# The same steps in another order: two layers of attention and feed-forward on one core, the start's transfers planned anew

## The chip, the core and the metric

One core of a Trainium2 chip. The core's engines are TensorE (PE, with its weight loads shown as PEld), VectorE (DVE), ScalarE (ACT), GpSimd (POOL) and SyncE (SP); each runs its own list of instructions, and they meet at semaphores. The metric is the device time of one execution in microseconds; of the kernel before three runs are shown, 415.20, 415.71 and 416.52, median 415.71.

## What is computed

Four sequences (batches) of 256 rows with 256 features, in float32, go through four stages. LN is a layer norm without parameters, and every stage adds its result to `x`.

```
x += softmax(LN(x) ctx^T / 16, masked) ctx                     ctx: 1601 rows per batch
x += top-2 of 8 experts, weighted: (silu(h Wg) * (h Wu)) Wd    h = LN(x), chosen by softmax(h Wr)
x += softmax(the 54 largest of coef (LN(x) Wq^T) ctx^T) ctx Wo^T
x += bitlinear(gelu(bitlinear(LN(x), w1)), w2)                 8-bit activations, ternary weights
```

## The kernel before, in words

The 1,024 rows are eight tiles `t` of 128 rows (two to a batch). `ctx` is cut in four column chunks `c` for scores and in four units `u` (three of 512 rows, one of 65) for the product with the values. `x` is loaded and normalised in pairs of tiles, the rows `u` of `ldx`, `stats`, `norm` and `xT`.

The whole program is one list, `ORDER`, of steps such as `s1.0.2`. Each engine's block walks this list and emits the steps that are its own; a step of another engine is passed over. So the list fixes the order of each engine's instructions, and nothing else does: the semaphore waits are worked out from it (`n(op, *key)` is the number of steps of that name up to this one). The rings of buffers follow the list too: two score banks (`s1`, `s3`, `up`), two transpose banks, one bank `O` for all small products, one accumulator `A`.

The steps that matter here, with their lines:

- On SP, all in list order through one queue: `ldx.u` (L468, 256 KB of x), `ldk.l.b.c` (L484, 400 KB of transposed ctx: layer l, batch b, chunk c; for b above 0 it waits until both tiles of the batch before have used that chunk), `ldv.l.a.u` (L502, 512 KB of ctx rows, 65 KB for the last unit), `fixed` (L470 to L473: two weight matrices and four scalars), `zero` (L476, fills the 1,920 KB DRAM array `xs` with zeros), `wg`, `wd` (L527, L534, expert weights), `xgl` (L510, loads a tile of gathered rows), `yst` (L515, stores an expert's output).
- On ACT, which also issues some loads: the first mask (L627) and the router weights (L628) ahead of the list, `mask.b` (L637, turns the byte mask into an additive one; then it issues the next batch's mask load, L641), `wload` (L706, L709), `wqa` (L720, mean magnitude of a weight matrix), `xTe`, `pTe` (L655, L670, copies out of a transpose bank), `exp1`, `exp3` (L661, L751), `egap` (L696), `qTe` (L729), `silu`, `ye`, `xgTe`, `gelu`, `gmul`, `aTe`, `cent`, `h4e`. Exponential, silu and gelu need different tables, and a change of table is an ACT_TABLE_LOAD.
- On TensorE: `xT`, `pT`, `xgT`, `q4`, `h4T` (transposes), `s1.t.c` and `s3.t.c` (scores, L905; the bank must be free, that is the `s1e` two chunks earlier must be done), `pvm.l.t.u` (values, L932 for layer 1, L936 for layer 3), `router`, `rank`, `GU`, `down` (experts), `wqs` (L999), `qT`, `wo`, `up`, `dn`.
- On VectorE: `stats`, `aggr`, `var`, `norm`, `s1e` (L1106, adds the mask and keeps the maximum), `max1`, `x1` (L1126), `rt1`, `rt2`, `pos` (routing), `mul` (L1197), `upd` (L1218), `wqb` (L1235 to L1243, the weight quantisation), and for layer 3 the search for the 54-th largest score: `pairH`, `pairL` fold a row of 1601 in two halves, `maxH`, `repH`, `maxL`, `repL` (L1260 to L1277) take eight values at a time out of each half, `merge`, `thr` find the threshold, `cut` (L1296) applies it; `x3` (L1312), `xabs` (L1318), `gabs`, `fin` (L1365).
- On POOL: the constants, `rstd` (L576), `scat` (L586, scatters the rows to `xs` by expert, only when `zero` has landed), `gat` (L597, gathers the experts' outputs, only when all `yst` have landed).

The rows of a batch of layer 1 wait for its mask: the first `s1e` of tile 0 needs `mask.0`. In `wqa` and `wqb` the array `w_raw` is rows 2 and 3 of `row3`.

Of the kernel before, what the change touches and what calls it, by code (L numbers as in the profile page):

```python
# [18 lines left out]
P = 128  # L19
# [54 lines left out]
fixed exp1.1 pvm.1.0.1 pT.1.0.2 ldv.1.0.3 pTe.1.0.2 s1.2.2 pT.1.1.0 ldk.3.0.0 pT.1.0.3 pvm.1.0.2 pTe.1.1.0 s1e.2.2  # L74
s1e.2.0 pT.1.1.1 s1.2.1 pTe.1.1.1 pTe.1.0.3 coef_e rstd.1.3 ldk.3.0.3 s1e.2.1 s1.3.1 pvm.1.0.3 r1.0 pT.1.1.2 pT.1.1.3
s1.2.3 x1.0 s1e.2.3 s1e.3.1 pvm.1.1.0 max1.2 s1.3.2 ldk.1.2.2 pvm.1.1.1 s1e.3.2 pTe.1.1.2 pTe.1.1.3 pvm.1.1.2
ldv.1.1.0 s1.3.0 pvm.1.1.3 x1.1 ldk.1.2.1 ldv.1.1.3 ldv.1.1.1 stats.2.0 exp1.2 aggr.2.0 pT.1.2.0 s1.3.3 var.2.0
pTe.1.2.0 s1e.3.0 s1e.3.3 xT.1.2 pT.1.2.1 max1.3 pvm.1.2.0 pTe.1.2.1 ldv.1.1.2 ldv.3.0.3 ldk.1.2.0 xTe.1.2 mask.2
rstd.2.0 s1.4.1 pT.1.2.2 exp1.3 ldk.1.2.3 pTe.1.2.2 pvm.1.2.1 norm.2.0 s1.4.2 pT.1.2.3 s1e.4.2 pTe.1.2.3 s1e.4.1
pvm.1.2.2 pT.1.3.0 pT.1.3.1 r1.1 pvm.1.2.3 norm.1.3 pTe.1.3.0 pTe.1.3.1 s1.4.3 pT.1.3.2 x1.2 wload.2 pTe.1.3.2 s1e.4.3  # L80
pvm.1.3.0 pT.1.3.3 s1.4.0 pvm.1.3.1 s1e.4.0 max1.4 xT.2.0 pvm.1.3.2 ldv.1.2.2 pTe.1.3.3 ldv.1.2.1 exp1.4 pvm.1.3.3
wqa.2 s1.5.3 x1.3 ldk.1.3.3 stats.2.1 aggr.2.1 xTe.2.0 ldv.1.2.0 var.2.1 s1e.5.3 router.0 pT.1.4.0 s1.5.1 rstd.2.1
norm.2.1 s1.5.0 ldk.1.3.0 rt1.0 s1e.5.1 xT.2.1 pTe.1.4.0 ldk.1.3.1 s1e.5.0 s1.5.2 s1e.5.2 ldk.1.3.2 xTe.2.1 pT.1.4.1
ldv.1.2.3 router.1 rt1.1 xT.1.3 max1.5 pvm.1.4.0 rank.0 mask.3 pTe.1.4.1 pos.0 xTe.1.3 pT.1.4.2 pT.1.4.3 pTe.1.4.3
pvm.1.4.1 s1.6.2 exp1.5 scat.0.0 scat.1.1 wg.0.0 pTe.1.4.2 s1e.6.2 pT.1.5.0 pT.1.5.1 wd.0.0 egap.0 pvm.1.4.2 scat.3.0
rt2.0 wqs.2 r1.2 pTe.1.5.0 pT.1.5.2 pvm.1.4.3 s1.6.0 ldk.3.0.2 wg.0.1 x1.4 scat.0.1 scat.2.1 scat.1.0 pTe.1.5.1
scat.3.1 wd.0.1 pT.1.5.3 s1e.6.0 pTe.1.5.2 wg.0.2 pvm.1.5.0 s1.6.1 s1.7.1 pvm.1.5.1 s1e.6.1 scat.2.0 xgl.0.0 pvm.1.5.2
s1.6.3 xgT.0.0 s1e.7.1 xgl.0.1 ldv.1.3.0 xgl.0.2 pTe.1.5.3 pvm.1.5.3 wqb.2 xgT.0.1 xgTe.0.0 GU.0.0 xgTe.0.1 x1.5
xgT.0.2 stats.2.2 xgl.0.3 wd.0.2 aggr.2.2 var.2.2 xgl.0.5 rstd.2.2 silu.0.0 ldv.1.3.2 mul.0.0 GU.0.1 norm.2.2 s1e.6.3
s1.7.3 xgl.0.4 silu.0.1 s1e.7.3 ldv.1.3.1 mul.0.1 max1.6 xgTe.0.2 xgT.0.3 down.0.0 xgTe.0.3 GU.0.2 wg.0.3 xgl.0.6  # L90
xgT.0.5 ye.0.0 down.0.1 wd.0.3 silu.0.2 wg.0.4 xgT.0.4 xgTe.0.4 xgl.0.8 mul.0.2 ye.0.1 wd.0.4 GU.0.3 silu.0.3 down.0.2
yst.0.0 xgTe.0.5 wg.0.5 ye.0.2 mul.0.3 s1.7.2 GU.0.4 wd.0.5 exp1.6 yst.0.1 xgl.0.7 wg.0.6 down.0.3 yst.0.2 wd.0.6
xgT.0.6 xgl.0.9 silu.0.4 xgTe.0.6 ye.0.3 GU.0.5 silu.0.5 wg.0.7 mul.0.4 down.0.4 xgT.0.7 wd.0.7 pT.1.6.0 ye.0.4
mul.0.5 GU.0.6 xgTe.0.7 down.0.5 pTe.1.6.0 wg.0.8 xgT.0.8 xgTe.0.8 silu.0.6 yst.0.3 yst.0.4 ye.0.5 mul.0.6 GU.0.7
wd.0.8 xgl.0.11 xgl.0.10 xgT.0.9 xgTe.0.9 wg.0.9 yst.0.5 silu.0.7 down.0.6 wd.0.9 xgl.0.13 GU.0.8 mul.0.7 ye.0.6
s1e.7.2 s1.7.0 xgT.0.11 wg.0.10 down.0.7 xgl.0.12 silu.0.8 s1e.7.0 wd.0.10 GU.0.9 max1.7 wg.0.11 xgTe.0.11 mul.0.8
xgT.0.10 ye.0.7 silu.0.9 xgTe.0.10 pT.1.6.1 down.0.8 yst.0.6 egap.1 GU.0.10 yst.0.7 wd.0.11 mul.0.9 ye.0.8 down.0.9
exp1.7 wg.0.12 wd.0.12 GU.0.11 silu.0.10 pTe.1.6.1 mul.0.10 pT.1.6.2 wg.0.13 ye.0.9 xgT.0.12 down.0.10 xgl.0.14
silu.0.11 yst.0.8 xgTe.0.12 ye.0.10 mul.0.11 GU.0.12 wd.0.13 pTe.1.6.2 silu.0.12 wg.0.14 yst.0.9 xgT.0.13 xgTe.0.13
mul.0.12 down.0.11 GU.0.13 wd.0.14 xgT.0.14 ye.0.11 ldk.3.0.1 silu.0.13 down.0.12 xgTe.0.14 yst.0.10 ldv.1.3.3 rt2.1  # L100
yst.0.11 GU.0.14 mul.0.13 ye.0.12 down.0.13 silu.0.14 yst.0.12 pT.1.7.0 mul.0.14 ye.0.13 coef pT.1.6.3 down.0.14 r1.3
yst.0.13 ye.0.14 yst.0.14 pvm.1.6.0 pTe.1.7.0 pvm.1.6.1 xT.2.2 xTe.2.2 pvm.1.6.2 gat.0.0 pTe.1.6.3 ldv.3.0.0 gat.1.0
pvm.1.6.3 router.2 x1.6 gat.0.1 pT.1.7.1 upd.0.0 rt1.2 pT.1.7.2 gat.1.1 pvm.1.7.0 upd.1.0 upd.0.1 pTe.1.7.1 gat.2.0
pT.1.7.3 upd.1.1 pTe.1.7.3 pTe.1.7.2 pvm.1.7.1 gat.3.0 egap.2 stats.3.0 pvm.1.7.2 aggr.3.0 var.3.0 rstd.3.0 upd.2.0
norm.3.0 gat.3.1 pvm.1.7.3 upd.3.0 gat.2.1 x1.7 xT.3.0 xTe.3.0 stats.2.3 qT.0 aggr.2.3 var.2.3 rstd.2.3 upd.3.1 qTe.0
norm.2.3 upd.2.1 xT.2.3 s3.0.2 xTe.2.3 stats.3.1 aggr.3.1 var.3.1 router.3 rt2.2 s3e.0.2 s3.0.1 rt1.3 rank.1 rstd.3.1
s3e.0.1 norm.3.1 s3.0.0 s3.0.3 pos.1 xT.3.1 egap.3 scat.4.0 s3e.0.0 wg.1.0 rt2.3 scat.7.1 s3.1.2 ldk.3.1.2 s3e.0.3
pairH.0 s3e.1.2 s3.1.3 s3.1.0 scat.4.1 scat.7.0 pairL.0 maxH.0.0 xTe.3.1 s3e.1.3 maxL.0.0 ldk.3.1.0 repH.0.0 s3.1.1
repL.0.0 ldk.3.1.1 ldk.3.1.3 maxH.0.1 scat.5.0 scat.5.1 qT.1 s3e.1.1 s3e.1.0 scat.6.1 wd.1.0 qTe.1 maxL.0.1 s3.2.0
wg.1.1 s3.2.1 s3e.2.0 s3.2.3 pairH.1 s3e.2.1 s3.2.2 scat.6.0 repL.0.1 s3e.2.3 repH.0.1 wd.1.1 maxH.1.0 nmax.1 maxH.0.2  # L110
xgl.1.0 pairL.1 repH.1.0 repH.0.2 s3e.2.2 xgl.1.1 s3.3.0 xgl.1.2 maxL.1.0 maxH.0.3 xgT.1.0 xgl.1.3 maxH.1.1 xgT.1.1
xgTe.1.0 wg.1.2 xgl.1.4 xgTe.1.1 GU.1.0 xgT.1.2 GU.1.1 wd.1.2 repH.0.3 wg.1.3 ldk.3.2.0 repH.1.1 silu.1.0 xgT.1.3
mul.1.0 xgTe.1.2 s3.3.3 repL.1.0 xgl.1.5 xgTe.1.3 down.1.0 silu.1.1 maxH.0.4 ye.1.0 maxL.1.1 xgT.1.4 mul.1.1 xgl.1.6
wd.1.3 GU.1.2 repH.0.4 down.1.1 silu.1.2 maxH.1.2 mul.1.2 xgTe.1.4 nmax.0 GU.1.3 ye.1.1 xgT.1.5 wg.1.4 wd.1.4 down.1.2
# [1279 lines left out]
```

## Time and profile before

| | |
|---|---|
| runs, median (lowest to highest) | 415.71 us (415.20 to 416.52) |
| the profiled execution | 416.91 us |
| its span, first to last instruction | 415.2 us |
| mean granted TensorE clock | 0.971 |
| DMA over the span | 76.39 MB, mean 184 GB/s |
| instructions | 6,609 |

A row of a timeline has the start in us from the span's start, the duration in us, the engine, the line, the operation, what it writes and reads, the shapes, and how many instructions were merged in it; in brackets stands how long the engine was idle before it and what ended that. An engine with a q behind its name is its queue, issuing. Matmul ends are modelled. A row of groups has the busy time in us, the mean duration in ns of one, and the idle time before them.

### The profile page before, as it was taken

To read this page: it belongs to the slowest core of one execution; us is meant where nothing else is said; L and a number is where in the kernel's file an instruction comes from. 1 tells how busy PE (TensorE), PEld (TensorE's weight loads), DVE (VectorE), ACT (ScalarE), POOL (GpSimd) and SP (SyncE) were. 2 spreads that over 40 slices of the span, in tenths; PEclk is the share of its full clock that TensorE was granted. 3 is DMA by queue.
4 is the path that set the end of the run, shared out by engine and by line. 5 is a ranking of instruction groups with operands and counts; after the bars stand their busy time and mean duration, and the time that the engine had idled before them with its cause. 6 is when DMAs were issued, how large, how long until landed. Compare 5 with 4: busy or idle time off the path is not lost. (4 is left out here: it accounts for less than half of the span.)

```text
span 415.2 us, 6609 instructions
## 1 busy us (share of the span) xinstructions
PE 354.7 (85%) x2075; PEld 281.2 (68%) x2082; DVE 287.1 (69%) x701; ACT 186.9 (45%) x338; POOL 55.7 (13%) x132
## 2 busy tenths in 40 slices
PE   1899999999999999898998998879976754578884
PEld 1367778786888888564887997755953642567762
DVE  2363242745312124799798999999999998999843
ACT  1353254441373733232336373535555365543495
POOL 3100000052000005452000000451001002000110
PEclk9999999999999999998999999999999988689899
DMA  7978363857999974148797998651540230133311
GB/s 228 381 234 265 129 213 103 306 164 253 315 298 302 306 223 134 32 149 297 223 304 250 276 326 263 199 176 39 178 146 15 64 109 13 51 108 103 100 35 51
DMA packets 70810, 76.39 MB, mean 184 GB/s; under 512 B 5356, under 2 KB 69496, under 8 KB 70776
## 3 DMA queue, kind: packets, MB, share of 16 engines
q1 hardware_dynamic: 65912, 67.80, 51.9%
q0 software_dynamic: 1536, 4.20, 3.0%
q10 hardware_dynamic: 3328, 3.97, 2.8%
q8 instruction: 17, 0.28, 0.3%
q14 instruction: 17, 0.14, 0.1%
HBM read 66.91 MB, written 9.04 MB: 183 GB/s over the span
## 5 line engine op out<-in xcount | busy, mean ns | idle before, releaser
L983 PE MATMUL GU<-xgT,wg_ring 128*128 128x128 f32 x480 | 59.2, 276 | 2.8 <-ACT xgT L677 1.6
L983 PEld LDWEIGHTS GU<-xgT,wg_ring 128*128 128x128 f32 x480 | 56.8, 192 | 6.4 <-issue 3.3
L670 ACT ACTIVATE pT<-T 128x512 f32<-128x512 f32 (+1 forms) x64 | 32.1, 513 | 61.7 <-PE T L919 46.7
L936 PE MATMUL A<-pT,v_sb 128*128 128x128 f32 (+1 forms) x416 | 56.3, 293 | 3.9 <-DMA v_sb<-ctx 2.1
L936 PEld LDWEIGHTS A<-pT,v_sb 128*128 128x128 f32 (+1 forms) x416 | 53.4, 207 | 7.8 <-issue 3.9
L1260 DVE MAX8 cand_h<-fold 128x8 f32<-128x801 f32 x56 | 54.4, 983 | 0.0
L905 PE MATMUL S<-k_sb,xT 128*128 128x400 f32 (+2 forms) x128 | 50.8, 531 | 3.8 <-DMA k_sb<-ctxT 3.4
L905 PE MATMUL S<-k_sb,qT 128*128 128x400 f32 (+2 forms) x128 | 49.0, 528 | 4.0 <-DMA k_sb<-ctxT 1.9
L932 PE MATMUL A<-v_sb,pT 128*128 128x256 f32 (+1 forms) x208 | 49.0, 379 | 0.0
L1272 DVE MATCH_REPLACE8 fold<-cand_h,fold 128x801 f32<-128x801 f32 x48 | 46.9, 978 | 0.0
L1106 DVE CUSTOM_DVE_ANT_0 row<-S,mask_add 128x400 f32<-128x400 f32 (+2 forms) x32 | 18.1, 574 | 38.3 <-PE S L905 29.4
L919 PE MATMUL T<-ident,row 128*128 128x128 f32 (+1 forms) x208 | 32.7, 282 | 12.4 <-DVE row L1296 7.0
L932 PEld LDWEIGHTS A<-v_sb,pT 128*128 128x128 f32 (+1 forms) x208 | 38.2, 190 | 6.7 <-issue 0.4
L905 PEld LDWEIGHTS S<-k_sb,qT 128*128 128x128 f32 x128 | 24.5, 200 | 21.1 <-issue 6.4
L1197 DVE TENSOR_TENSOR hid<-hid,GU 128x256 f32<-128x256 f32 x30 | 12.6, 418 | 36.9 <-ACT hid L684 36.9
L919 PEld LDWEIGHTS T<-ident,row 128*128 128x128 f32 (+1 forms) x208 | 25.3, 146 | 18.9 <-issue 10.3
L905 PEld LDWEIGHTS S<-k_sb,xT 128*128 128x128 f32 x128 | 24.6, 202 | 19.2 <-DMA k_sb<-ctxT 5.0
L993 PE MATMUL O<-wd_ring,hid 128*128 128x256 f32 x120 | 31.2, 383 | 1.8 <-ACT y_sb L691 1.7
L1267 DVE MAX8 cand_l<-fold 128x8 f32<-128x801 f32 x32 | 31.4, 984 | 0.0
L597 POOL DMA_INDIRECT yg<-ys,idx_u x16 | 15.7, 981 | 88.7 <-DMA ys<-y_sb 83.2
L740 ACT ACTIVATE row<-S 128x400 f32<-128x400 f32 (+2 forms) x32 | 15.9, 503 | 24.7 <-PE S L905 24.7
L993 PEld LDWEIGHTS O<-wd_ring,hid 128*128 128x128 f32 x120 | 20.6, 190 | 4.8 <-ACT y_sb L691 2.8
(157 smaller groups left out, 460.3 us busy)
## 6 DMA issues: line engine op xcount, KB each, us to landing
v_sb<-ctx SPq DMA_DIRECT2D x36, 512.0 KB, 4.2
wg_ring<-Wg SPq DMA_DIRECT2D x30, 256.0 KB, 3.4
wg_ring<-Wu SPq DMA_DIRECT2D x30, 256.0 KB, 4.3
wd_ring<-Wd SPq DMA_DIRECT2D x30, 256.0 KB, 4.2
k_sb<-ctxT SPq DMA_DIRECT2D x16, 400.0 KB, 5.0
xg<-xs SPq DMA_DIRECT2D x30, 128.0 KB, 3.7
ys<-y_sb SPq DMA_DIRECT2D x30, 128.0 KB, 4.3
k_sb<-ctxT SPq DMA_DIRECT2D x8, 402.0 KB, 5.2
```

Of the source, the lines that this page charges most:

```text
L670: act.activation(pT[0:r, i % NPT, :, :].rearrange("p a s -> p (a s)")[:, 0:w], t_bank("pT", *key)[0:r, 0:w], ACT.Copy).then_inc(pTe_done, 1)
L740: act.activation(row3[:, t % 4, c0:c0 + w], s_bank("s3", t, c)[:, 0:w], ACT.Copy) \
L905: mm = pe.matmul(s_bank(*step)[:, 0:w], lhs[:, k, :], k_sb[:, l // 2, c, k, 0:w], start=k == 0, stop=k == KC - 1)
L919: mm = pe.transpose(t_bank(*step)[0:r, a * P:(a + 1) * P], src[:, m * P:m * P + r], ident[:, :])
L932: mm = pe.matmul(A_bank[:, 0:D], pT[0:r, j, a, :], v[0:r, a, :], start=m == 0, stop=m == NMC - 1)
L936: mm = pe.matmul(A_bank[:, o * P:(o + 1) * P], v[0:r, a, o * P:(o + 1) * P], pT[0:r, j, a, :], start=m == 0 and o == 0, stop=m == NMC - 1 ...
L983: mm = pe.matmul(gu_bank(*key)[:, a * F + f * P:a * F + (f + 1) * P], wg_ring[:, w % NWG, a, k, f * P:(f + 1) * P], cols[:, k, :], start=k ...
L993: mm = pe.matmul(O_bank[:, 0:D], hid[:, i % NHID, f, :], wd_ring[:, w % NWD, f, :], start=f == 0, stop=f == F // P - 1)
L1106: dve.tensor_tensor_reduce(out=row1[:, t % 2, c0:c0 + w], in0=s_bank("s1", t, c)[:, 0:w], in1=mask_add[:, c0:c0 + w], scale=1.0, scalar=BE ...
L1260: dve.max(cand_h[:, t % 2, 8 * r:8 * r + 8], fold[:, t % 2, 0:HALF]).then_inc(maxH_done, 1)
L1267: dve.max(cand_l[:, t % 2, 1 + 8 * r:9 + 8 * r], fold[:, t % 2, HALF:RW]).then_inc(maxL_done, 1)
L1272: dve.match_replace(part, cand_h[:, t % 2, 8 * r:8 * r + 8], part, BELOW_ALL).then_inc(repH_done, 1)
```

## The change

All steps of `ORDER` stand in another order; the set of steps is the same. One load is moved outside the list: the router weights are issued behind the conversion of the first mask instead of ahead of the list.

```diff
         def _(act):
             act.wait_ge(x_in[0], 16)
             act.dma_start(mask_u8[:, :], mask[0:1, :].partition_broadcast(P)).then_inc(mask_in, 16)
-            act.dma_start(wr_sb[:, :, :], Wr.rearrange("(k p) e -> p k e", p=P)).then_inc(wr_in, 16)
...
                     act.activation(mask_add[:, 0:M], mask_u8[:, :], ACT.Copy, scale=-NEG, bias=NEG) \
                        .then_inc(mask_done, 1)
+                    if b == 0:
+                        act.dma_start(wr_sb[:, :, :], Wr.rearrange("(k p) e -> p k e", p=P)).then_inc(wr_in, 16)
```

The list's beginning, to the first steps of batch 1, before and after:

```diff
-ldx.0 stats.1.0 ldx.2 ldk.1.0.3 ldx.3 ldk.1.0.1 ldk.1.0.0 ldk.1.0.2 ldx.1 zero wload.1 aggr.1.0 var.1.0 rstd.1.0
-norm.1.0 ldv.1.0.0 stats.1.2 aggr.1.2 xT.1.0 xTe.1.0 s1.0.1 mask.0 s1e.0.1 ldv.1.0.1 s1.0.2 stats.1.1 s1.0.0 s1e.0.2
-wqa.1 aggr.1.1 var.1.1 stats.1.3 wqs.1 rstd.1.1 var.1.2 s1e.0.0 rstd.1.2 norm.1.1 s1.0.3 s1e.0.3 s1.1.2 aggr.1.3
-max1.0 s1e.1.2 s1.1.1 s1.1.0 exp1.0 pT.1.0.0 ldk.1.1.1 s1e.1.1 ldk.1.1.0 s1e.1.0 s1.1.3 ldk.1.1.2 xT.1.1 pTe.1.0.0
-ldv.1.0.2 s1e.1.3 pT.1.0.1 norm.1.2 xTe.1.1 max1.1 ldk.1.1.3 wqb.1 ldv.3.0.1 mask.1 pvm.1.0.0 var.1.3 pTe.1.0.1 s1.2.0
-fixed exp1.1 pvm.1.0.1
+ldx.0 stats.1.0 aggr.1.0 var.1.0 rstd.1.0 norm.1.0 xT.1.0 xTe.1.0 ldx.2 ldk.1.0.3 ldk.1.0.1 s1.0.1 ldk.1.0.2 s1.0.2
+mask.0 ldx.3 ldx.1 ldk.1.0.0 ldv.1.0.0 fixed stats.1.2 stats.1.1 s1e.0.1 ldv.1.0.1 s1.0.0 s1e.0.2 s1e.0.0 s1.0.3
+aggr.1.1 var.1.1 stats.1.3 s1.1.2 s1e.0.3 rstd.1.1 aggr.1.2 max1.0 norm.1.1 ldv.1.0.3 ldv.1.0.2 s1e.1.2 s1.1.1 s1e.1.1
+exp1.0 aggr.1.3 var.1.3 s1.1.0 ldk.1.1.0 pT.1.0.0 s1e.1.0 ldk.1.1.1 s1.1.3 s1e.1.3 pTe.1.0.0 ldk.1.1.3 xT.1.1 pT.1.0.1
+ldk.1.1.2 ldk.3.0.1 xTe.1.1 max1.1 exp1.1 pvm.1.0.0 var.1.2 rstd.1.2 pTe.1.0.1 s1.2.0
```

The places of the new list that are spoken of below (with what stands between):

```
pvm.1.1.3 pTe.1.2.0 s1.3.0 x1.1 s1.3.3 s1e.3.0 ldv.1.1.1 pT.1.2.1 stats.2.0 aggr.2.0 wqs.1 s1e.3.3 ldk.1.2.3 xT.1.2
xTe.1.2 pvm.1.2.0 pTe.1.2.1 wqb.1 mask.2 ldk.1.2.0 ldv.1.1.2 pT.1.2.2 ldv.1.1.3 zero ldv.3.0.1 pT.1.2.3 s1.4.1
pTe.1.2.3 var.2.0 max1.3 rstd.2.0 s1.4.2 exp1.3 wload.2 r1.1 pTe.1.2.2 pvm.1.2.1 s1e.4.1 pvm.1.2.2
...
down.0.12 xgTe.0.14 GU.0.14 yst.0.11 ye.0.12 mul.0.13 yst.0.12 ldv.1.3.1 down.0.13 pT.1.6.3 silu.0.14 mul.0.14
ye.0.13 pT.1.7.0 down.0.14 yst.0.13 ye.0.14 yst.0.14 gat.0.0 pvm.1.6.0 ldk.3.0.0 pTe.1.6.3 ldv.3.0.3 gat.0.1 pvm.1.6.1
...
norm.3.0 xT.3.0 gat.3.1 x1.7 xTe.3.0 stats.2.3 qT.0 aggr.2.3 var.2.3 rstd.2.3 upd.3.0 egap.2 qTe.0
...
aTe.4 ldv.3.5.1 s3.7.3 s3e.7.3 repL.5.2 ginv.2 wo.4 gmul.2 maxH.5.5 xdeq.3 x3.4 h4T.2 cent.4 repH.5.5 h4e.2
```

## Rows read from the trace of the kernel before

**Rows 1.** The page's parts 1 and 2, busy time and bandwidth by slice
```profile
PE 354.7 (85%) x2075; PEld 281.2 (68%) x2082; DVE 287.1 (69%) x701; ACT 186.9 (45%) x338; POOL 55.7 (13%) x132
...
GB/s 228 381 234 265 129 213 103 306 164 253 315 298 302 306 223 134 32 149 297 223 304 250 276 326 263 199 176 39 178 146 15 64 109 13 51 108 103 100 35 51
```

**Rows 2.** Windows by stage: length; busy PE, PEld, DVE, ACT, POOL; clock; DMA share; GB/s
```profile
0.00:30.00 30.00, 19.01 (x59) 11.03 (x59) 12.50 (x49) 9.77 (x10) 5.38 (x51) 1.00 0.85 278
30.00:180.30 150.30, 146.62 (x823) 118.45 (x824) 59.63 (x237) 62.00 (x118) 21.66 (x24) 1.00 0.66 213
180.30:393.20 212.90, 174.03 (x1069) 140.51 (x1073) 206.24 (x390) 98.62 (x187) 26.89 (x50) 0.94 0.53 164
393.20:415.20 22.00, 14.99 (x128) 11.19 (x128) 8.70 (x26) 16.55 (x26) 1.78 (x8) 0.99 0.16 54
```

**Rows 3.** Timeline of all engines, 0 to 30 us
```profile
9.69 3.03 PE L905 MATMUL S<-k_sb,xT 128*128 128x400 f32 x4 [1.37 <-DMA k_sb<-ctxT]
...
11.10 1.54 ACT L637 ACTIVATE mask_add<-mask_u 128x1601 bf16<-128x1601 uint8 x1 [2.15 <-DMA mask_u<-mask]
...
14.78 4.90 PE L905 MATMUL S<-k_sb,xT 128*128 128x400 f32 x8 [2.06 <-DMA k_sb<-ctxT]
...
22.29 1.63 ACT L661 ACTIVATE row<-row,nm 128x1601 f32<-128x1601 f32 x1 [4.15 <-DVE nm L1114]
```

**Rows 4.** Timeline of TensorE, 24 to 60 us
```profile
30.00 1.59 PE L905 MATMUL S<-k_sb,xT 128*128 128x402 f32 x4 [0.33 <-issue]
...
37.65 2.85 PE L905 MATMUL S<-k_sb,xT 128*128 128x400 f32 x8
...
45.73 3.61 PE L932 MATMUL A<-v_sb,pT 128*128 128x256 f32 x16
```

**Rows 5.** DMA issues of 0 to 30 us: KB each, median us to landing
```profile
v_sb<-ctx SPq DMA_DIRECT2D x4, 512.0 KB, 8.4
xs<-zeros SPq DMA_DIRECT2D x1, 1920.0 KB, 16.5
...
row<-w1T ACTq DMA_DIRECT2D x1, 1024.0 KB, 11.5
```

**Rows 6.** The tile k_sb, 0 to 30 us: DMA to landing
```profile
DMA to landing us min/median/max: 3.2/5.9/10.9
```

**Rows 7.** Timeline of VectorE, 28 to 60 us: the quantisation's passes
```profile
28.96 1.29 DVE L1241 TENSOR_SCALAR row<-row,wscl 128x2048 f32<-128x2048 f32 x1
...
31.55 1.23 DVE L1243 TENSOR_SCALAR w1q<-row 128x2048 bf16<-128x2048 f32 x1
```

**Rows 8.** Timeline of TensorE, 80 to 110 us
```profile
102.14 0.41 PE L967 MATMUL T<-ident,xg 128*128 128x128 f32 x2 [0.67 <-DMA xg<-xs]
```

**Rows 9.** Timeline of all engines, 150 to 182 us
```profile
150.64 4.81 SPq L515 DMA_DIRECT2D ys<-y_sb  x3
...
153.56 1.13 PE L993 MATMUL O<-wd_ring,hid 128*128 128x256 f32 x4 [0.20 <-ACT y_sb L691]
...
168.32 0.63 PE L890 MATMUL T<-ident,xn 128*128 128x128 f32 x4
...
171.75 0.69 ACT L729 ACTIVATE qT<-O,scal 128x512 f32<-128x512 f32 x1 [2.16 <-PE O L1009]
```

**Rows 10.** DMA issues of the whole run: KB each, median us to landing
```profile
v_sb<-ctx SPq DMA_DIRECT2D x36, 512.0 KB, 4.2
```

**Rows 11.** Timeline of ScalarE, 216 to 224 us
```profile
220.46 1.28 ACT L751 ACT_TABLE_LOAD   x1
221.76 1.63 ACT L751 ACTIVATE fold<-row,nmax 128x1601 f32<-128x1601 f32 x1
```

**Rows 12.** Timeline of VectorE, 199 to 226 us
```profile
223.49 1.89 DVE L1296 SCALAR_TENSOR_TENSOR row<-row,thr,fold 128x1601 f32<-128x1601 f32 x1 [1.33 <-ACT fold L751]
```

**Rows 13.** Timeline of VectorE, 340 to 347 us
```profile
341.56 0.47 DVE L1312 SCALAR_TENSOR_TENSOR x_res<-O,r,x_res 128x256 f32<-128x256 f32 x1
...
345.31 0.42 DVE L1318 TENSOR_REDUCE xabs<-xn 128x1 f32<-128x256 f32 x1 [1.34 <-ACT xn L765]
```

More of the change, by code:

```diff
@@ L74 @@
[L74 to L113, printed above, removed]
@@ L129 @@
-pTe.3.1.1 repL.2.2 ldv.3.1.3 down.1.13 ldk.3.2.3 silu.1.14 yst.1.12 rc3.1 mul.1.14 repH.3.0 ye.1.13 maxL.2.3 pT.3.1.2
-yst.1.13 down.1.14 ye.1.14 pvm.3.1.0 yst.1.14 ldv.3.1.2 maxH.2.6 repL.3.0 merge.2 maxH.3.1 thr.2 gat.4.0 maxL.3.1
-repH.3.1 repL.3.1 wo.0 pTe.3.1.2 pT.3.1.3 pvm.3.1.1 pvm.3.1.2 pTe.3.1.3 gat.5.0 maxH.3.2 exp3.2 cut.2.0 gat.4.1
-upd.4.0 x3.0 ldv.3.2.0 pvm.3.1.3 pT.3.2.0 upd.4.1 upd.5.0 repH.3.2 gat.5.1 upd.5.1 maxH.3.3 pT.3.2.1 aTe.1 sq4.0 wo.1
-gat.6.0 pTe.3.2.0 pTe.3.2.1 stats.3.2 gat.7.0 gat.6.1 upd.6.0 pvm.3.2.0 aggr.3.2 ldv.3.2.3 x3.1 var.3.2 cent.0 rc3.2
@@ new lines @@
+x1.0 pTe.1.1.0 s1e.2.3 s1.2.1 pTe.1.1.1 rstd.1.3 s1e.2.1 s1.3.1 pvm.1.1.0 max1.2 exp1.2 pT.1.1.2 s1.3.2 pTe.1.1.2
+pT.1.1.3 wqa.1 ldk.1.2.2 s1e.3.1 s1e.3.2 ldk.1.2.1 pvm.1.1.1 pT.1.2.0 pvm.1.1.2 ldv.1.1.0 pTe.1.1.3 pvm.1.1.3
+pTe.1.2.0 s1.3.0 x1.1 s1.3.3 s1e.3.0 ldv.1.1.1 pT.1.2.1 stats.2.0 aggr.2.0 wqs.1 s1e.3.3 ldk.1.2.3 xT.1.2 xTe.1.2
+pvm.1.2.0 pTe.1.2.1 wqb.1 mask.2 ldk.1.2.0 ldv.1.1.2 pT.1.2.2 ldv.1.1.3 zero ldv.3.0.1 pT.1.2.3 s1.4.1 pTe.1.2.3
+var.2.0 max1.3 rstd.2.0 s1.4.2 exp1.3 wload.2 r1.1 pTe.1.2.2 pvm.1.2.1 s1e.4.1 pvm.1.2.2 s1e.4.2 norm.2.0 pT.1.3.0
@@ new lines @@
+pTe.1.3.0 pvm.1.2.3 pT.1.3.1 pTe.1.3.1 s1.4.0 pT.1.3.2 s1e.4.0 s1.4.3 x1.2 pvm.1.3.0 s1e.4.3 pTe.1.3.2 max1.4 pT.1.3.3
+pTe.1.3.3 xT.2.0 pvm.1.3.1 ldv.1.2.0 wqa.2 coef_e exp1.4 ldk.3.0.3 pvm.1.3.2 ldv.1.2.1 pvm.1.3.3 s1.5.3 x1.3 stats.2.1
+s1.5.1 ldv.1.2.3 aggr.2.1 ldk.1.3.3 s1e.5.3 xTe.2.0 norm.1.3 ldk.3.0.2 s1.5.2 var.2.1 s1e.5.1 rstd.2.1 norm.2.1
+router.0 pT.1.4.0 ldv.1.2.2 xT.2.1 rt1.0 xTe.2.1 pTe.1.4.0 s1.5.0 router.1 s1e.5.2 ldk.1.3.1 xT.1.3 pvm.1.4.0 rt1.1
+xTe.1.3 s1e.5.0 ldk.1.3.0 rank.0 pT.1.4.1 pos.0 pT.1.4.2 mask.3 ldk.1.3.2 pTe.1.4.1 s1.6.0 s1.6.2 wg.0.0 scat.0.0
@@ new lines @@
+ye.1.14 repH.3.0 yst.1.14 pT.3.1.1 merge.2 repL.3.0 pTe.3.1.1 pT.3.1.2 pT.3.1.3 maxH.3.1 pvm.3.1.1 ldv.3.1.2 gat.4.0
+thr.2 maxL.3.1 ldk.3.2.1 gat.4.1 exp3.2 pTe.3.1.3 repH.3.1 wo.0 repL.3.1 gat.5.0 upd.4.0 pTe.3.1.2 ldv.3.2.0 gat.5.1
+x3.0 sq4.0 cut.2.0 pvm.3.1.2 va4.0 gat.6.0 maxH.3.2 upd.5.0 pvm.3.1.3 rs4.0 ldv.3.2.3 pT.3.2.0 aTe.1 pT.3.2.1
+pTe.3.2.0 upd.4.1 wo.1 ldv.3.2.1 gat.7.1 cent.0 upd.5.1 pvm.3.2.0 repH.3.2 stats.3.2 maxH.3.3 aggr.3.2 x3.1 gat.7.0
+ldk.3.2.3 var.3.2 pTe.3.2.1 repH.3.3 pvm.3.2.1 sq4.1 rstd.3.2 ldv.3.2.2 norm.3.2 maxH.3.4 xT.3.2 xTe.3.2 gat.6.1
@@ new lines @@
+maxL.3.2 pT.3.2.2 qT.2 repH.3.4 qTe.2 va4.1 pTe.3.2.2 rs4.1 s3.4.0 upd.6.0 maxH.3.5 repL.3.2 cent.1 s3e.4.0 xabs.0
+ldv.3.3.0 upd.6.1 pT.3.2.3 s3.4.1 s3.4.2 repH.3.5 upd.7.0 xabs.1 maxL.3.3 s3e.4.1 upd.7.1 s3e.4.2 s3.4.3 xmx.1
+maxH.3.6 xdeq.1 xmx.0 stats.3.3 pvm.3.2.2 s3e.4.3 merge.3 pairH.4 pTe.3.2.3 aggr.3.3 xinv.1 thr.3 rc3.2 maxH.4.0
+s3.5.1 var.3.3 pairL.4 exp3.3 rstd.3.3 xdeq.0 s3.5.0 cut.3.0 nmax.4 s3e.5.1 norm.3.3 pvm.3.2.3 repH.4.0 s3.5.2
+maxL.4.0 ldv.3.3.1 xinv.0 s3e.5.0 xT.3.3 s3.5.3 pT.3.3.0 s3e.5.3 ldv.3.3.3 maxH.4.1 xTe.3.3 aTe.2 pTe.3.3.0 ldk.3.3.1
```

124 lines of the change are left out of this document (75 added, 49 removed).

## The prediction

> **What bounds the kernel now.** The page's busy times come first [rows 1]: TensorE 85%, VectorE 69%, neither enough alone. The windows by stage split the run [rows 2]. From 30 to 180.3 us TensorE is busy 146.6 of 150.3 us while VectorE has 59.6: TensorE's list is the clock. From 180.3, where the first `pairH` (the start of the 54-th-largest search) stands, to 393.2 VectorE is busy 206.2 of 212.9 us. The last 22 us are a dependent tail in which neither is full. In the first 30 us the two are busy for only 19.0 and 12.5 us. So the time is: start, TensorE's list to `pairH.0`, VectorE's list to the last `xscl`, tail. Next I read the start's timeline and the transfers issued in it, because there the new list differs most, and last the idle times named at single instructions inside the two full stretches.
>
> At the start the reader sees TensorE wait for keys, run its first score chunk at 9.69, stop, and resume at 14.78, again behind keys [rows 3]. It runs cold: four products span 3.03 us and four more take about as long, while warm ones follow each other at about 1.34 (two take 2.85 with the last one's end, [rows 4]). The transfers explain it: beside the first batch's keys a 1,024 KB weight load went over ACT's queue and took 11.5 us to land, and behind them stood a 1,920 KB fill (16.5 us) [rows 5].
>
> **The change part by part.** Which step an instruction belongs to follows from the list, because each engine runs its steps in that order; I counted the instructions out of the trace and summed their steps again in the new order.
>
> (a) The sets. TensorE does the same steps ahead of its first `s3` in both lists, VectorE the same ones ahead of `pairH.0` and ahead of `merge.7`. No instruction count changes. So only idle time can change, and I go through the places where it can.
>
> (b) The start. New: `xT.1.0 s1.0.1 s1.0.2 s1.0.0 s1.0.3`, keys 1 and 2 are the fourth and fifth loads, the weight load and the fill are gone from this stretch. Chunk 1's keys now end 1,311 KB into SP's queue instead of 1,567; 256 KB at the 381 GB/s of [rows 1] are 0.7 us, so they land at about 9.0, not 9.7. Chunk `s1.0.1` then runs cold from 9.1 to 12.0, `s1.0.2` follows without a stop and warms on the way (old TensorE was at the short step about 3.9 us after 14.78), to 13.9. The mask's conversion (11.10 plus 1.54, [rows 3]) still opens the first `s1e` at 12.8 and its transfer is not moved, so the bank for `s1.0.0` is free at 13.4; `s1.0.0` ends 15.3, `s1.0.3` 16.6, `s1.1.2` 18.0. VectorE now holds things up: `s1e.0.0` (0.6), `aggr.1.1`, `var.1.1`, `stats.1.3` (1.2 together), `s1e.0.3` end at 17.8, then `aggr`, `max1.0`, `norm.1.1` (1.4) and `s1e.1.2` end at 19.7, and `s1.1.0` waits for this bank until 19.8. `exp1.0` needs 1.8 [rows 3] after `max1.0`, so `pT.1.0.0` starts at 21.1, and with one chunk, two transposes of 0.45 and so on `pvm.1.0.0` starts near 24.2 and ends at 25.9. `s1.2.0` needs batch 1's keys, sent when `s1.1.0` is done at 21.1; the quickest key transfer of the stretch took 3.2 us, the median 5.9 [rows 6]. The queue is empty by then, I take 3.2 to 4.5: `s1.2.0` starts at 25.9 instead of 30.00 [rows 4]. The old list had also run `wqs.1` (0.5) by then, so the head start is 4.1 - 0.5 = **3.6 us**. Bounds: 5.0 if VectorE's pieces overlap better, 1.3 if TensorE stays cold for one chunk more (1.3) and the keys take 5.9 (about 1 more).
>
> (c) The weight quantisation `wqb.1` moves from 28.5 us, where VectorE was idle afterwards, to between `s1e.3.3` and `max1.3`. Its three passes take 1.29, 1.23 and 1.23 [rows 7], about 4.3 with the small ones. TensorE has from the end of `s1.3.3` to `pvm.1.2.2`: two full groups of transposes, one of a single tile and an `xT` (1.4), two value units of 1.72 (two take 3.61 in [rows 4]), two chunks of 1.34, `wqs` 0.15, together 7.7. The chain: a 0.3 us late `s1e.3.3` (0.6), `wqb.1` 4.3, `var` and `max1.3` 0.5, `exp1.3` 1.8, `pTe` 0.6, four hand-overs 0.5: 8.7. **Cost 1.0 us**; bounds 0 and the whole 4.3.
>
> (d) Smaller waits of the same kind in the new list ahead of `rank.0`: `s1.3.1` behind `x1.0` and `s1e.2.3` (0.3), `s1.5.2` behind `x1.3`, `stats`, `aggr`, `s1e.5.3` (0.2 over before): **0.5**. New waits of 0.4 to 0.5 between `rank.0` and `xgT.0.0` cost nothing: there eight scatters end at a landing for which TensorE waited before too [rows 8], and TensorE's work between is 17.4 instead of 17.1 us. In the feed-forward stretch `egap.0` and `egap.1` and one exp stand together ahead of `silu.0.10`: **0.4**. Bounds for (d) together: 0 and 2.
>
> (e) The fill, now sent near 50 us, stands behind all keys and values of its neighbourhood, and its first user, the scatters, come 30 us later; the transfers were at two thirds of their time there [rows 2]. Its cover is that distance; 16.5 us would still fit. `wload.1` has no user before `wqa.1`. Cost 0. Router weights: one 8 KB load goes behind the mask's conversion; it has 50 us until `router.0`, and the second mask's load behind it has over 10. Cost 0. SP now issues `fixed` (six loads) ahead of values 1, 3 and 2; SP has nothing due until 21 us.
>
> (f) Behind `down.0.14` (153.56 plus 1.1) the path runs over the store, the gathers, `upd`, `norm.3.0` to `xT.3.0` at 168.32 [rows 9]; TensorE's own work between is as long, 13.5 us, in both lists. New is that `ldv.1.3.1` (512 KB) is sent behind `yst.0.12`, at old times 151.1, with the stores of [rows 9]. With the 4.2 us that value loads usually take [rows 10] it lands at 155.3, before `pvm.1.6.1` at 156.0. Cost 0; upper bound below. Also new: `egap.2` with its table load stands between `xTe.3.0` and `qTe.0`. A load of 1.28 [rows 11] and 0.2 for `egap` fit into the 2.16 us for which ACT waited ahead of `qTe.0` [rows 9]. The Trainium skill says otherwise: "ScalarE: Activation LUTs", What ACT_TABLE_LOAD costs, gives every switch a drain of about 1.38 us beside the load's 1.28. By that `qTe.0` would come 0.7 us later and the sum would be 2.0 faster instead of 2.7; here the exponential begins right at the load's end (220.46 + 1.28, 221.76), so the trace does not agree. The new list has 20 such loads instead of 18; ACT is busy 98.6 of 212.9 us [rows 2] and the two lie off VectorE's path.
>
> (g) VectorE's full stretch. The distance of every `mul`, `cut`, `gabs` and `xabs` from what it waits for is within 0.5 us of before up to `cut.0.0`, whose wait of 1.33 stays [rows 12]. The wait of 1.34 at 345 [rows 13] and one of 0.37 behind it came from `x3.4` (341.56) standing just 2.7 us of VectorE work ahead of `xabs.4`; now 8.5 stand between. In return `aTe.4` comes behind two exponentials, and `x3.4` is wanted 5.6 us sooner. I take **1.0 gained** of the 1.7; bounds 1.7 and a loss of 1. The tail has the same chain, `wo.7 cent.7 h4e.4` to `dn.7`: 0, with 0.7 either way.
>
> Sum: -3.6 + 1.0 + 0.5 + 0.4 - 1.0 = -2.7 us. The profiled execution took 416.91 (span 415.2), 1.2 above the median of 415.71; the sum is a difference, so profiled 414.2 and median **413.0**.
>
> **The rivals.** *1, all of it arrives.* TensorE reaches `wqb.1` with its waits taken up by others, and both waits at 345 go: -3.6 - 1.7 = -5.3, 410.4. For: small waits seldom add. Against: VectorE has no slack around `wqb.1`. 15%. *2, the start gives little.* Keys or cold TensorE as in the bound of (b): -1.3 + 1.9 - 1.0 = -0.4, 415.3. For: every load there takes longer than later, 8.4 against 4.2 us for values [rows 5, 10]. 20%. *3, slower: the late value load.* If `ldv.1.3.1` takes the 8.4 us of [rows 5] it lands 3.5 us after `pvm.1.6.1` is due, and as TensorE's work there is as long as the path, all 3.5 count: -2.7 + 3.5 = +0.8, and with 0.5 for the last store and gathers queued behind it +1.3, 417.0. It decides above 4.9 us from issue; the gain is gone at 7.6. The transfers are near full in the stretch before. 13%. *4, the switch.* If a table load keeps ACT twice as long as its row (2.56), `qTe.0` is 0.6 late: 413.6. 5%. "ScalarE: Activation LUTs" of the Trainium skill is the page that would have it so. The forecast itself has 47%, with 410.9 to 415.0 as its own range.
>
> **How the numbers follow.** Faster by over 0.3% (1.25 us, about what a measurement of this kernel can tell from no change): 0.42 of the forecast, rivals 1 and 4, 0.02 of rival 2: 0.64. Within: 0.04 + 0.16 = 0.20. Slower: 0.01 + 0.02 + 0.13 = 0.16. Range 410.5 to 416.6: it holds the forecast, rivals 2 and 4 and the near half of 1.
>
> **What the new profile would show.** (b) right: TensorE's second chunk without a stop at 12, `s1.2.0` near 26. (c) right: a wait of about 1 us of the transposes' copy for `exp1.3` near 55. `pairH.0` near 178.6 instead of 180.3, the end of VectorE's stretch near 390.5. Wrong if TensorE still stops for keys after its first chunk, if `pvm.1.6.1` waits for v_sb, or if `xabs.4` still waits.

## The result, and the profile after

| | before | after |
|---|---|---|
| runs of this comparison, median (lowest to highest, 20 each) | 417.3 us (415.18 to 421.72) | 412.98 us (409.18 to 419.04) |
| ratio after to before, 95% interval | | 0.9881 (0.9857 to 0.9905) |
| the profiled execution, its span | 416.91 us, 415.2 us | 413.82 us, 412.1 us |
| mean granted TensorE clock | 0.971 | 0.959 |
| ACT busy, table loads | 186.9 us, 18 | 190.4 us, 20 |

The changed kernel is 1.2% faster: 0.0119 of 417.3 is 5.0 us. The ratio leaves disturbed runs out, so it is not quite the quotient of the two medians, 0.9896. The two profiled executions differ by 3.1 us only. The one of before took 0.4 less than its median, the one of after 0.8 more, so the traces show the direction of each part better than its size.

A second profiled execution of the changed kernel (called the second trace below; it is the run new_again) had a span of 410.3. Windows of the first one, cut where the same steps stand as in [rows 2] (columns as there):

```profile
0.00:30.00 30.00, 22.00 (x78) 14.11 (x79) 10.41 (x44) 10.54 (x12) 6.03 (x52) 1.00 0.79 250
30.00:175.80 145.80, 141.35 (x803) 115.02 (x802) 60.90 (x241) 60.68 (x116) 21.39 (x23) 1.00 0.70 225
175.80:389.80 214.00, 175.33 (x1079) 141.70 (x1084) 206.25 (x391) 103.33 (x187) 30.43 (x51) 0.93 0.51 164
389.80:412.10 22.30, 15.34 (x119) 10.84 (x119) 8.63 (x26) 15.87 (x25) 1.55 (x7) 0.92 0.13 44
```

The first `pairH` stands at 175.8 instead of 180.3. TensorE's idle time from 30 us to it is 4.45 us (145.80 less 141.35), before it was 3.68 [rows 2]. So the stretch that TensorE's list sets is not shorter, it only begins earlier, and the gain was made in the first 25 us. From `pairH` to the start of the last-but-one `xscl` it is 214.0 us where before it was 212.7 (that `xscl` starts at 393.0; the window of [rows 2] is cut 0.2 behind it). The tail, 22.3 from there, was 22.2, but its clock is 0.92 where it was 0.99.

TensorE's start (timeline of the changed kernel; the answer to [rows 3] and the second row of [rows 4]):

```profile
9.09 11.62 PE L906 MATMUL S<-k_sb,xT 128*128 128x400 f32 x28 [0.78 <-ACT xT L656]
...
24.92 1.51 PE L906 MATMUL S<-k_sb,xT 128*128 128x402 f32 x4
```

Seven chunks run as one row from 9.09, where before TensorE stopped for keys at 12.7 and began again at 14.78. The second chunk's first weight load is at 11.2 and `s1.2.0`, the second row, at 24.9 (its weight load at 24.7), against 30.00. The end of the list has a new wait on VectorE, for `x3.6`:

```profile
384.18 0.48 DVE L1313 SCALAR_TENSOR_TENSOR x_res<-O,r,x_res 128x256 f32<-128x256 f32 x1 [1.76 <-PE O L1018]
```

The wait at `xabs.4` [rows 13] is gone: in the timeline of the changed kernel it follows at once on what stands ahead of it.

```profile
340.61 0.17 DVE L1286 TENSOR_TENSOR split_min<-cand_h,cand_l 128x28 f32<-128x28 f32 x1
340.70 0.41 DVE L1319 TENSOR_REDUCE xabs<-xn 128x1 f32<-128x256 f32 x1
```

### The profile page after: what moved, and what is told of

Same layout as the page of the kernel before. It is cut to its first block, busy times and chain, and to the rows that moved or that the text cites. A ratio compares the mean times of both kernels' runs of the same rounds, so it can differ in the third digit from the quotient of the medians.

```text
span 412.1 us, 6611 instructions
## 1 busy us (share of the span) xinstructions
PE 354.0 (86%) x2075; PEld 281.7 (68%) x2082; DVE 286.2 (69%) x701; ACT 190.4 (46%) x340; POOL 59.4 (14%) x132
## 4 chain that ended last, share of the span: by engine, by line
PE 43%; DVE 23%; issue 12%; DMA 11%; SPq 4%; POOL 3%; ACT 3%; POOLq 0%; ACTq 0%; DVEq 0%
PE S L906 11%; PE GU L984 8%; PE A L933 8%; DVE fold L1273 5%; DVE cand_h L1261 5%; PE O L994 4%; DMA ys<-y_sb 4%; PE T L920 3%; DMA xs<-xn,idx_u 3%; PE A L937 2%; POOL xs L586 2%; DVE cand_l L1268 2%; DMA xg<-xs 2%; DVE fold L1278 2%; SPq L527 2%
## 5 line engine op out<-in xcount | busy, mean ns | idle before, releaser
L906 PE MATMUL S<-k_sb,xT 128*128 128x400 f32 (+2 forms) x128 | 48.3, 518 | 0.8 <-ACT xT L656 0.8
L920 PE MATMUL T<-ident,row 128*128 128x128 f32 (+1 forms) x208 | 33.7, 286 | 10.1 <-DVE row L1297 9.8
L906 PEld LDWEIGHTS S<-k_sb,qT 128*128 128x128 f32 x128 | 23.4, 196 | 21.9 <-ACT row L741 5.9
L920 PEld LDWEIGHTS T<-ident,row 128*128 128x128 f32 (+1 forms) x208 | 26.1, 148 | 16.9 <-issue 12.7
L906 PEld LDWEIGHTS S<-k_sb,xT 128*128 128x128 f32 x128 | 24.2, 198 | 15.9 <-issue 3.2
L741 ACT ACTIVATE row<-S 128x400 f32<-128x400 f32 (+2 forms) x32 | 15.9, 502 | 25.2 <-PE S L906 25.2
```

The source lines that it names most:

```text
L906: mm = pe.matmul(s_bank(*step)[:, 0:w], lhs[:, k, :], k_sb[:, l // 2, c, k, 0:w], start=k == 0, stop=k == KC - 1)
L920: mm = pe.transpose(t_bank(*step)[0:r, a * P:(a + 1) * P], src[:, m * P:m * P + r], ident[:, :])
```

## The experiments

All twelve were timed in five rounds against the kernel before, in three groups, each on one chip. The order is that of the questions. Where a kernel is said to differ in "places", these are places in the one list of steps; no step is added or left out anywhere.

**Where was it made?** First the changed kernel once more.

> The changed kernel itself, timed beside the splices on one chip. If the ratio of its first measurement holds, 0.988; if the gap between its two profiled executions (3.1 us) is the truth, 0.9925. In either case its first pairH stands near 175.8 us; what a second trace can tell is whether TensorE's clock drops again in the last 10 us.

Measured: 412.11 us, ratio 0.9874 (0.9816 to 0.9931), where the kernel before has a median of 418.39. `pairH.0` at 175.4, and the clock fell again at the end. The result holds.

Then the two lists were spliced. The first half of the first pair:

```diff
-(old list)
+(new list up to s1.2.0) (the rest of the old list in its own order)
```

> New list up to s1.2.0, then the old list's remaining steps in the old order; router weights as in the new kernel. Theory A (all of the gain is made in the first 25 us and carried through TensorE's full stretch): s1.2.0 near 24.7, the first pairH near 175.5 to 176, and a time 4 to 5 us below the kernel before. Rival B (the gain comes from the rest of the list, and a head start is given back at the next wait): pairH near 179 to 180, 0 to 1.5 us below.

Measured: 424.37 us, ratio 1.0133 (1.0085 to 1.0180), slower than both. `s1.2.0` was at 24.8, so the start was won. Then TensorE stood still (its timeline, the only row with a wait from 24 to 62 us):

```profile
34.22 0.59 PE L1000 MATMUL O<-wabs,ones 128*128 128x2 f32 x2 [7.73 <-ACT gel L721]
```

The steps that the new start puts off, the weight load, its mean and its sum `wqs.1`, came first in the rest, so TensorE waited 7.73 us for a matrix that had only just been asked for. The splice was made badly for my question; what it does show is that a head start lasts to the first step whose input was put off further than the step itself.

The other half:

```diff
-(new list)
+(old list up to s1.2.0) (the rest of the new list in its own order)
```

> Old list up to s1.2.0, then the new list's remaining steps in the new order. Theory A: s1.2.0 stays at 30.0, the first pairH comes at 180 to 181, and the time is within 1 us of the kernel before, or up to 1.5 us slower because the new order behind pairH has about 1.3 us more waits. Rival B: 2 to 4 us faster.

Measured: 417.15 us, ratio 0.9977 (0.9936 to 1.0017): no change that can be told from none. `s1.2.0` was at 28.0 in this trace and `pairH.0` at 178.2, 150.2 us behind it, where the kernel before has 150.3. By itself the new order behind the start gives at most 2.7 us, by the interval's lower end, and in the trace nothing ahead of `pairH.0`.

That `s1.2.0` stands at 28.0 here and not at 30.0, with the same list up to it, matters for what the start is worth. The stop for keys is there too, but the two chunks behind it took 2.96 us, where they took 4.90 before [rows 3] (TensorE's timeline):

```profile
14.09 2.96 PE L905 MATMUL S<-k_sb,xT 128*128 128x400 f32 x8 [1.78 <-DMA k_sb<-ctxT]
```

So 1.9 of the 5.3 us between 30.0 and 24.7 are TensorE's slow pace behind the stop in that one trace of the kernel before, and not the stop.

A splice at a place where both lists have done nearly the same steps:

```diff
-(old list)
+(new list up to s1.4.2) (the rest of the old list in its own order)
```

> The splice made again where the two lists agree better: new list up to s1.4.2 (with the weight load, its mean and its quantisation at the new places, 6 us of TensorE's work after s1.3.3), the old order behind it. Theory A (the gain is the start): s1.2.0 near 25, first pairH near 176 to 177, pairH to last-but-one xscl 212 to 213, time 4 to 5 us below the kernel before, within 1 us of the changed kernel. Rival B (the gain needs the new order of the feed-forward stretch): pairH at 178 or later and at most 2 us below the kernel before.

Measured: 418.14 us, ratio 1.0017 (0.9976 to 1.0057). By its numbers this is rival B, by the place of the loss it is not. `s1.2.0` at 25.2 and `s1.4.1` at 51.3 are those of the changed kernel, and `pairH.0` is at 179.8; but already `router.1`, ahead of the feed-forward stretch, stands at 78.8 where the kernel before has 80.1, so that of the 4.8 us won 1.3 are left. TensorE's timeline, the window over it (columns of [rows 2]) and ScalarE's timeline show the larger part of the loss:

```profile
70.91 1.03 PE L947 MATMUL O<-wr_sb,xT 128*128 128x8 f32 x8 [1.14 <-issue]
...
72.53 4.28 PE L906 MATMUL S<-k_sb,xT 128*128 128x400 f32 x8
```

```profile
66.00:82.00 16.00, 14.86 (x74) 10.82 (x73) 7.61 (x40) 7.05 (x10) 0.69 (x1) 0.89 0.66 223
```

```profile
68.33 1.91 ACT L721 ACTIVATE gel<-row 128x2048 f32<-128x2048 f32 x1 [1.46 <-DMA row<-w2T]
70.14 0.19 ACT L721 ACTIVATION_READ_ACCUMULATOR gel<-row 128x1 f32 x1
70.24 0.58 ACT L656 ACTIVATE xT<-T 128x512 f32<-128x512 f32 x1
```

The first router product waited 1.14 us (1.8 counted from the last weight load) for ScalarE's copy of `xT`, which stands behind the mean of the second weight matrix, and that one waited 1.46 us for its load. The splice sends this load at 59.3, when the moved fill (50.3 to 61.3) was still under way, and it landed at 68.3, 9 us later; the kernel before sends it at 63.1 and has it at 68.4, the new list sends it at 53.1. And behind that stop the granted clock of the stretch is 0.89 and the eight products of a chunk pair take 4.28 us, where eight take 2.85 in [rows 4]: 1.4 us more. Together that is 3.2 us of the 4.3 by which the way from `s1.2.0` to `pairH.0` is longer than before (154.6 against 150.3).

Last of this group, only the second half of the run in the old order:

```diff
-(new list)
+(new list up to s3.0.2) (the rest of the old list in its own order)
```

> New list up to s3.0.2, the old order behind it. Theory A (the new order of VectorE's stretch and of the tail is worth nothing or costs about 1.3 us): first pairH near 175.8, then old behaviour, 393.0 - 180.3 = 212.7 us from pairH to the last-but-one xscl as before, so 0 to 1.5 us below the new kernel in the traces, 411 to 412 us. Rival C (the new order behind pairH has gained, as the prediction's step (g) said by 1.0): 1 us above the new kernel.

Measured: 413.21 us, ratio 0.9871 (0.9812 to 0.9929), where the changed kernel beside it has 412.11 and 0.9874. The two can't be told apart, but each interval reaches 2.4 us either way, so the runs rule out neither the 1 us of gain of rival C nor as much of loss. What they do show is that the gain over the kernel before does not need the new order of VectorE's stretch and of the tail.

**What made the start short?** The first try put both bulk transfers back:

```diff
-ldx.3 ldx.1 ldk.1.0.0 ldv.1.0.0
+ldx.3 ldx.1 zero wload.1 ldk.1.0.0 ldv.1.0.0
```

> The new list with the 1,920 KB fill and the 1,024 KB weight load put back behind the start's loads of x, all else new. Theory S (the bulk transfers share the wires with the keys and hold SP's queue, and that is what made the old start long): the mask, keys 0 and the first values land 2 to 4 us later than in the new kernel, s1.0.0 or pvm.1.0.0 waits, s1.2.0 comes at 27 to 29 instead of 24.7 to 25.5, time 2 to 4 us above the new kernel. Rival K (the order of the keys alone made the gain, since TensorE needs keys 3 and 1 first): s1.2.0 stays within 1 us of 25, time within 1 us of the new kernel.

Measured: 423.58 us, ratio 1.0154 (1.0101 to 1.0208), `s1.0.0` at 22.3 and `s1.2.0` at 34.8. It overshoots, because the fill now stood ahead of keys 0 in SP's queue, which it did not in the old list. So again, with the fill behind the keys and the weight load at the head of ACT's list:

```diff
-ldx.0 stats.1.0
+ldx.0 wload.1 stats.1.0
...
-ldk.1.0.0 ldv.1.0.0
+ldk.1.0.0 zero ldv.1.0.0
```

> The new list with the weight load at its very start on ACT's queue, as before, and the fill behind the last of the first batch's keys (ahead of values 0). The first try had put the fill ahead of keys 0, which the old list did not. Theory S (bulk beside the keys makes the start long): keys 1 and 2 land 1 to 4 us later, TensorE stops for them as in the old kernel, values 0 land 4 us or more late, s1.2.0 at 27 to 30 and the time 2 to 4 us above the new kernel. Rival K (the order of the keys made the gain): s1.2.0 within 1 us of 25.2.

Measured: 416.64 us, ratio 1.0005 (0.9964 to 1.0046). With the order of the new list and the bulk where it was, no gain is left that the ratio can show. (By the medians of all runs, 416.64 against 418.39 of the kernel before, 1.7 us of it may be.) Within this group it is 3.3 us slower than `tail_mended`, 413.33, which is the changed kernel but for six steps near the end. TensorE's timeline:

```profile
9.11 5.35 PE L906 MATMUL S<-k_sb,xT 128*128 128x400 f32 x8 [0.78 <-ACT xT L656]
16.27 7.00 PE L906 MATMUL S<-k_sb,xT 128*128 128x402 f32 x20 [1.82 <-DVE mx1c L1107]
...
28.87 1.59 PE L906 MATMUL S<-k_sb,xT 128*128 128x402 f32 x4 [1.22 <-issue]
```

Keys 1 and 2 were in time, so the old stop behind the first chunk does not come back: that half of theory S failed, the new order of the loads alone is enough against it. But TensorE started its third chunk 2.7 us late (16.3 against 13.6 in the run below), and `s1.2.0` came at 28.8. The row says that the third chunk waited for VectorE's release of its bank. VectorE's timeline tells why:

```profile
14.98 0.75 DVE L1071 BATCH_NORM_STATS2 bn<-x_res 128x6 f32<-128x256 f32 x2 [7.22 <-DMA x_res<-x]
15.65 0.56 DVE L1107 CUSTOM_DVE_ANT_0 row<-S,mask_add 128x400 f32<-128x400 f32 x1
```

`stats.1.1`, which stands ahead of `s1e.0.1`, waited for rows 1 of `x`, landed at 14.96 beside the weight load (12.30 without it, in the run below), and the bank's reader could only follow. Keys 0 landed at 16.05 instead of 13.39, so they would have held the chunk as long. SP's own timeline shows the second half of it:

```profile
5.48 0.57 SPq L476 DMA_DIRECT2D xs<-zeros  x1
6.10 9.75 SPq L502 DMA_DIRECT2D v_sb<-ctx  x1
15.89 1.81 SPq L470 DMA_DIRECT2D wq_sb<-WqT  x1
...
23.30 2.67 SPq L484 DMA_DIRECT2D k_sb<-ctxT  x4
```

The issue of values 0 behind the fill took 9.75 us, and all that SP had to send stood behind it. In the changed kernel the same issue takes 0.48:

```profile
5.27 0.48 SPq L502 DMA_DIRECT2D v_sb<-ctx  x1
...
20.73 3.17 SPq L484 DMA_DIRECT2D k_sb<-ctxT  x5
```

The fill alone:

```diff
-ldk.1.0.0 ldv.1.0.0
+ldk.1.0.0 zero ldv.1.0.0
```

> The new list with the fill alone put back, behind keys 0 and ahead of values 0; the weight load stays late. If the weight load beside the keys is what stops TensorE's second chunk, this run starts as the new kernel does (s1.0.2 at 11.2), and only values 0 and what SP sends behind them are late: pvm.1.0.0 waits for v_sb. If the values land by 24 all the same, s1.2.0 stays within 1 us of 25.2 and the time within 1 us of the new kernel.

Measured: 414.33 us, ratio 0.9944 (0.9910 to 0.9978): 2.3 us faster than with both put back, 1.0 slower than `tail_mended` in the same group.

```profile
9.11 11.51 PE L906 MATMUL S<-k_sb,xT 128*128 128x400 f32 x28 [0.78 <-ACT xT L656]
...
26.82 1.59 PE L906 MATMUL S<-k_sb,xT 128*128 128x402 f32 x4 [1.83 <-issue]
```

```profile
6.70 6.53 SPq L502 DMA_DIRECT2D v_sb<-ctx  x1
...
20.65 3.50 SPq L484 DMA_DIRECT2D k_sb<-ctxT  x5
```

The first seven chunks are those of the changed kernel (values 0, landed at 21.0, were in time). What is late are the keys of batch 1: sent at the same time, 20.65, they landed 6.1 us later (26.73) instead of 3.3, because the 1.1 MB of values sent from 17.8 on, and not from 11.3, stood ahead of them. `s1.2.0` is at 26.8 after a wait of 1.83 us. So of the 3.6 us by which `s1.2.0` fell behind with both put back, the fill makes some 1.6 and the weight load beside the keys the other 2.

The converse, the bulk alone taken out of the old start:

```diff
-ldx.1 zero wload.1 aggr.1.0
+ldx.1 aggr.1.0
...
+mask.1 wload.1
...
-ldv.1.1.3 ldv.1.1.1
+ldv.1.1.3 zero ldv.1.1.1
```

(and `wqa.1`, `wqs.1`, `wqb.1` between the steps that they stand between in the new list)

> The old list with the weight load behind mask.1, the fill behind ldv.1.1.3, and the mean, the sum and the quantisation of that weight behind it as in the new list; keys, loads of x and all else as in the old one. Theory S: the start loses its stop for keys, s1.2.0 at 25 to 27 instead of 28 to 30, and the time is 2 to 4 us below the kernel before. Rival K: s1.0.2 still waits (x 2 and 3 and the keys' order are as before), s1.2.0 at 28 or later.

Measured: 423.28 us, ratio 1.0172 (1.0111 to 1.0234). The start does what theory S says: `s1.0.2` at 12.6 instead of 14.8, `s1.2.0` at 26.2. The time does not follow, for two waits of TensorE for values:

```profile
39.55 0.70 PE L932 MATMUL A<-v_sb,pT 65*128 65x256 f32 x2 [2.52 <-DMA v_sb<-ctx]
...
60.45 1.99 PE L932 MATMUL A<-v_sb,pT 128*128 128x256 f32 x8 [3.66 <-DMA v_sb<-ctx]
```

The first was sent behind `ldv.3.0.1` and `fixed` in SP's queue, with the weight load beside them, the second, `ldv.1.1.1`, behind the fill, where my edit had put it. In the new list the fill goes out at 49.8, lands at 63.5, and the only load close behind it is one of layer 3. (Its issue holds SP from 50.3 to 55.8; nothing else is due.) Putting a bulk transfer off is half of the work; the other half is a place with nothing due behind it.

**Was the quantisation's place worth 1.0 us?**

```diff
-pTe.1.2.1 wqb.1 mask.2
+pTe.1.2.1 mask.2
...
-exp1.3 wload.2 r1.1
+exp1.3 wload.2 wqb.1 r1.1
```

> The new list with the weight quantisation moved on VectorE's list from ahead of max1.3 to behind it, ahead of r1.1. By the prediction's step (c), which priced its place at 1.0 us: exp1.3 starts some 3 us earlier, pTe.1.2.2 near 52.5 instead of 54.7, pvm.1.2.2 up to 1.0 us earlier, pairH.0 up to 1.0 earlier. Rival (TensorE's steps between cover nearly all of it): pairH.0 moves by less than 0.4 us, since only 0.4 us of idle time of TensorE stand there in the trace. Against a gain: s1e.4.1 and s1e.4.2 now stand behind the 4.3 us and the score bank comes free later, so s1.4.0 may wait.

Measured: 412.51 us, ratio 0.9872 (0.9830 to 0.9914), the same as the changed kernel. `pvm.1.2.2` came 0.5 us earlier than in the second trace, from the same 25.5 of `s1.2.0`, and `pairH.0` 0.8 later, at 176.3. So the place did not cost 1.0 us of time; but `pairH.0` moved by more than the 0.4 of the rival, and the wrong way, and from `s1.2.0` to it four traces of one and the same list spread more than that (149.8 to 151.1 us), so how little the place costs is read from TensorE's idle time and not from `pairH.0`.

**Can the waits behind `pairH` be had?**

```diff
-silu.1.0 mul.1.0 xgl.1.6 silu.1.1 xgT.1.3 down.1.0 maxH.1.1 mul.1.1 xgTe.1.2 GU.1.2 maxH.0.4
+silu.1.0 xgl.1.6 silu.1.1 xgT.1.3 down.1.0 maxH.1.1 mul.1.0 xgTe.1.2 GU.1.2 maxH.0.4 mul.1.1
...
```

(`mul.1.6` behind `pairH.2`, `mul.1.14` behind `maxH.2.6`, `cut.2.0` ahead of `upd.4.0` likewise)

> The new list with four mul (1.0, 1.1, 1.6, 1.14) each put one VectorE step later and cut.2.0 one place earlier, ahead of upd.4.0, so that a step which is ready stands where VectorE waited. In the new kernel's two traces these five places have 5.2 and 3.6 us of waits. If VectorE's list is the clock of this stretch, pairH.0 to merge.7 falls from 204.7 and 203.4 to about 200 to 201 and the time by 2.5 to 4 us. Rival: the waits come back at the next dependent step (TensorE's or ACT's chain is as long), and less than 1 us is left.

Measured: 414.03 us, ratio 0.9930 (0.9895 to 0.9965), not better than the changed kernel. `pairH.0` to `merge.7` is 202.6 us against 204.7, 203.4 and 202.5 in three traces of the unedited stretch. The wait at `mul.1.0` is gone and one of 0.89 stands at `mul.1.5`:

```profile
210.71 0.42 DVE L1198 TENSOR_TENSOR hid<-hid,GU 128x256 f32<-128x256 f32 x1 [0.89 <-ACT hid L685]
```

And the new wait for `x3.6`:

```diff
-pT.3.6.2 (as before) pTe.3.6.2 maxL.7.3 pvm.3.6.2 pT.3.6.3 ldv.3.7.0 maxH.7.6 ldv.3.7.1 up.3.0
+pT.3.6.2 pT.3.6.3 (as before) pTe.3.6.2 pTe.3.6.3 maxL.7.3 pvm.3.6.2 ldv.3.7.0 maxH.7.6 ldv.3.7.1
...
-wo.6 cut.7.0 gelu.3.0 rc3.6 cut.7.1 pT.3.7.0 x3.6
+wo.6 up.3.0 cut.7.0 gelu.3.0 rc3.6 cut.7.1 pT.3.7.0 cut.7.2 cut.7.3 x3.6
```

(and `ldv.3.6.2` ahead of `ldv.3.6.3`)

> The new list with six steps near its end moved: the transpose and copy of the last unit of tile 6 up behind the third, up.3.0 behind wo.6, ldv.3.6.2 one place up, cut.7.2 and cut.7.3 ahead of x3.6. In four traces of the new order VectorE waits 1.6 to 1.8 us for x3.6 in three, and TensorE waits 0.5 to 0.6 us for values there. If steps out of place make that wait, x3.6 stands 1 us earlier and the wait is filled: the last-but-one xscl comes 1.5 us earlier and the end 0.9 to 1.5 us earlier than in the new kernel. Rival (TensorE's clock makes it: the wait was missing in the one trace in which the values' products of tile 6 ran at the full clock): pvm.3.6.0 takes 3.1 us where the clock is halved and 1.9 where not, in this kernel too, and the gain is at most half of that.

Measured: 413.33 us, ratio 0.9928 (0.9896 to 0.9959). VectorE no longer waits for `x3.6`; from `cut.6.0` to the last-but-one `xscl` it is 20.6 us instead of 21.9, but from `cut.6.0` to the last `fin` 41.2 instead of 41.5: given back in the tail. Here TensorE's clock comes in beside the list. The same stretch, 366 to 376 us, of the second trace of the changed kernel and of wqb_behind_exp, whose lists differ only in where `wqb.1` stands, near 50 us (windows; columns of [rows 2]):

```profile
346.00:366.00 20.00, 12.47 (x72) 11.21 (x72) 20.00 (x37) 8.74 (x11) 0.22 (x1) 0.75 0.26 82
366.00:376.00 10.00, 8.29 (x50) 7.38 (x49) 10.00 (x19) 3.84 (x9) 0.90 (x3) 0.66 0.09 21
```

```profile
346.00:366.00 20.00, 12.41 (x71) 11.16 (x72) 20.00 (x38) 8.75 (x11) 0.22 (x1) 0.75 0.27 82
366.00:376.00 10.00, 7.70 (x63) 6.71 (x62) 10.00 (x19) 3.83 (x9) 0.90 (x3) 1.00 0.26 69
```

Both had 0.75 in the 20 us before; then one stretch was granted 0.66, the other 1.00. The value products of tile 6 in it, and the wait that follows:

```profile
370.67 3.07 PE L937 MATMUL A<-pT,v_sb 128*128 128x128 f32 x16
```

```profile
369.42 2.02 PE L937 MATMUL A<-pT,v_sb 128*128 128x128 f32 x16
```

```profile
382.37 0.48 DVE L1313 SCALAR_TENSOR_TENSOR x_res<-O,r,x_res 128x256 f32<-128x256 f32 x1 [1.61 <-PE O L1018]
```

```profile
380.60 0.48 DVE L1313 SCALAR_TENSOR_TENSOR x_res<-O,r,x_res 128x256 f32<-128x256 f32 x1
```

Sixteen products took 3.07 us at the lower clock and 2.02 at the full one, and VectorE's wait of 1.61 us is there in the one and absent in the other. The other traces bear it out: in all seven in which the new tail stands and `pvm.3.6.0` takes 2.8 to 3.1 us from its first weight load to its last, the wait is 1.6 to 1.9; here both are absent (1.67). So in the new tail the wait comes with the clock. In `tail_mended` those products took 2.24, between the two, so its missing wait is not the list's alone. What the old tail would do with slow products there is not shown: in its traces they all took 1.67. None of the twelve kernels is clearly faster than the changed one.

## Why the prediction came out as it did

**The number.** 412.98 lies on the forecast of 413.0, but partly by luck. The forecast was 2.7 us less than 415.71, the median of three runs; of twenty runs the kernel before has 417.3. The gain is 5.0 us by the ratio (4.0 to 6.0 by its interval) and was undersized by about two.

**(a)** No work was added or taken away. TensorE is busy 354.0 us against 354.7, VectorE 286.2 against 287.1. Only idle time moved.

**(b), the start.** The mechanism is right and the size is off: 3.6 expected; 24.7 instead of 30.0, less `wqs.1`, is 4.8 in the profiled pair, inside the bound of 5.0. In eight traces with the new start `s1.2.0` has its weight load at 24.4 to 25.5, and the old start gave 30.0 and, in rest_only, 28.0, so 2.5 to 5.6 before the 0.5 of `wqs.1`. The 30.0 that I reckoned from held 1.9 us of slow products behind the stop, which `rest_only` has not; against 28.0 the head start is 2.0 to 3.1, below the forecast. Two traces of the old start do not tell which of them is the usual one, nor, with that, where all of the 5.0 us of the runs lie. On the new side each link was too long by a little. The first chunk was put at 2.9 us, and took 2.1 up to the second one's start (11.2). It took no longer before: behind 14.78 the second chunk's first weight load is at 16.95, 2.2 later. The row's 3.03 us run to the last product's modelled end and are not the distance to the next chunk. VectorE's pieces let `s1.1.0` begin at 19.1 rather than 19.8; the keys of batch 1 took 3.3 us, the low end of the 3.2 to 4.5 taken. From 9.1 the weight loads follow at 0.67 us and from 13.1 at 0.33, as before behind 14.78 and from 18.9; the windows show a granted clock of 1.00 all through, so this halving is read from the loads and not from the clock's column. What the prediction did not separate is what makes the start short, the order of the keys or the missing bulk. The runs do: the bulk's removal takes away a wait of 2.7 us (for rows 1 of `x`, and for keys 0 as well) and SP's 9.75 us at one issue, and with the bulk back and the new order the ratio is that of before. The order of the loads alone takes the stop for keys away, and no gain in time came with it.

**(c), the quantisation, and (d).** Mis-sized: 1.0 and 0.9 of loss expected, 0 to 0.8 found (TensorE's idle time between 30 us and `pairH.0` grew by 0.77 in one trace; `s1.2.0` to `pairH.0` is 151.1 and 149.9 against 150.3, with `wqs.1` now in it). Both ends of the comparison were off. The chain, put at 8.7 us from the end of `s1.3.3`, took 7.9 to the end of the copy `pTe.1.2.2` (47.33, where TensorE turns to its next weights, to 55.26). TensorE, put at 7.7, took 8.5 to the first weights of `pvm.1.2.2` (55.83). Its timeline (changed kernel) runs past the spot without a stop, and the copy's exponential starts in time:

```profile
49.28 1.96 PE L933 MATMUL A<-v_sb,pT 128*128 128x256 f32 x8 [0.40 <-issue]
...
54.31 3.61 PE L933 MATMUL A<-v_sb,pT 128*128 128x256 f32 x16
```

```profile
53.05 1.63 ACT L662 ACTIVATE row<-row,nm 128x1601 f32<-128x1601 f32 x1 [0.89 <-DVE nm L1115]
```

The one stop, 0.40 ahead of `pvm.1.2.0`, is for the copy behind `xTe.1.2` and not for the quantisation. So the copy was done 0.6 us before TensorE came to it. I should have set the chain against TensorE's whole time between the two steps, with the stops that it has there anyway, and not against its work alone.

**(e)** Right: the fill, sent at 49.8, landed at 63.5 and no first user waited; that it holds SP for 5.5 us was not foreseen and cost nothing there. The router weights and the second mask were hidden.

**(f)** Right, both. Rival 3's late value load landed 3.9 us after its issue (4.9 was the limit), and `pvm.1.6.1` follows `down.0.14` by 2.5 us as before. `egap.2` with its table load fitted in (ScalarE's timeline, the answer to the last row of [rows 9]):

```profile
165.09 1.28 ACT L697 ACT_TABLE_LOAD   x1
166.39 0.20 ACT L697 ACTIVATE egap<-gap 128x2 f32<-128x2 f32 x1
167.24 0.69 ACT L730 ACTIVATE qT<-O,scal 128x512 f32<-128x512 f32 x1 [0.65 <-PE O L1010]
```

The load's 1.28 us are followed by its activation 0.02 later, and ScalarE still waited 0.65 for TensorE. The drain of 1.38 us at each switch that the Trainium skill gives ("ScalarE: Activation LUTs", What ACT_TABLE_LOAD costs) does not show: with it `qTe.0` would have been late.

**(g), VectorE's stretch.** Half right. The waits of 1.34 and 0.37 at `xabs.4` and `fin.2` went, and `pairH.0` to `merge.7` shrank from 205.4 to 204.7 and 203.4. (The wait at `cut.0.0`, which I had left at 1.33, is 0.18 and 0.92, and `mul.1.6`, which had none, has 1.66 and 0.53.) What I missed is behind it: from `merge.7` to the last-but-one `xscl` 7.2 us became 9.3, of it 1.76 the wait for `x3.6`. The distance is thin there: from the start of `cut.6.0` VectorE has 14.7 us of work ahead of `x3.6`, and TensorE's chain took 16.5 in this trace and at most 14.6 in wqb_behind_exp. It takes TensorE's lower clock to make it a wait, and the prediction had priced no clock. The step's gain of 1.0 was a loss of 1.3 in the profiled pair, a gain of 0.1 in the second trace (212.6 us from `pairH.0` to that `xscl`) and of 2.7 in wqb_behind_exp (210.0), where the clock was full; the runs can't tell it from nothing (new_half_old_half). The step looked at VectorE's distance ahead of `xabs.4` and not at the one ahead of `x3.6`, and so missed that its sign hangs on TensorE's clock.

**The tail** was put at 0 and is 0 by the sum, 19.5 and 19.6 us from that `xscl` to the last `fin`. Inside, the low clock has moved. Before, it lay under the value products of tile 7 at 388.8, which took 2.98 us. After, it lies under the last two products of the run (TensorE's timeline, before and after):

```profile
409.77 1.03 PE L1049 MATMUL O<-w2q,gelT 128*128 128x256 bf16 x8 [0.30 <-ACT gelT L808]
411.38 1.05 PE L1049 MATMUL O<-w2q,gelT 128*128 128x256 bf16 x8 [0.58 <-DVE fin L1365]
```

```profile
405.39 1.72 PE L1050 MATMUL O<-w2q,gelT 128*128 128x256 bf16 x8 [0.30 <-ACT gelT L809]
407.68 1.67 PE L1050 MATMUL O<-w2q,gelT 128*128 128x256 bf16 x8 [0.58 <-DVE fin L1366]
```

**The rivals.** Rival 1 gave 5.3 and lies nearest to the ratio's 5.0, but not for its reasons: the start gave more than it had in the profiled pair, and the second half, which was to give 1.7, took 1.3 in it and gave 0.1 in the second trace. Rival 2 (the start gives little) and 4 are out. Rival 3's price did not arise, though its mechanism, a value load behind a bulk transfer, cost two waits of 2.5 and 3.7 us in old_without_bulk, where I had put one there myself.

## What to carry to other kernels

In the first microseconds count what shares the wires and the queue with the transfers that the first products need, not only the order of those: two transfers, 2.9 MB together, that could wait 20 us cost this kernel 3.3 us by the medians within one group of runs, 2.3 of it the 1 MB beside the first keys, and by the ratios all of the 1.2% gained. When they are put off, look at what stands behind them in the new place and how far away its first user is, since three of the kernels tried lost the head start again at exactly such a step (`start_only`, `start_then_old`, `old_without_bulk`). And set a chain against the whole time of the busiest engine between its two ends, with the stops and the clock that it has there already.

## What was not expected of the hardware

- **An issue can hold its queue's engine.** Behind the fill, one `dma_start` of values held SP for 9.75 us (6.53 with the weight load gone, 5.49 in the fill's new place), against 0.48 without the fill. In the start the engine was free again only some 6 us before the fill landed (15.9 and 21.8; 13.2 and 19.4). It is not always so: in old_without_bulk, where the fill landed after 8.2 us, the issue behind it took 1.8.
- **A stop can have a low clock behind it, and a longer one none.** Start_then_old has 0.89 over the 16 us that hold its stop of 1.1 us, and 4.28 us for eight products that take 2.85; the kernel before, without the stop, has 1.00 from 66 to 82 us. Behind the 7.73 us of start_only the clock is 0.51 from 30 to 40 us. But in old_without_bulk it is 1.00 around the stops of 2.52 and 3.66 us (window over the second, columns of [rows 2]), and in fill_back_behind_keys around the one of 1.83. So the length of the stop does not decide it, and what does stays open.

```profile
56.00:66.00 10.00, 6.34 (x32) 4.81 (x30) 4.21 (x12) 2.48 (x4) 0.00 (x0) 1.00 0.84 268
```

- **The same list is granted different clocks.** Over the twenty runs of the changed kernel the mean granted clock is 0.951 to 0.974, and the fastest run, 409.18 us, has the highest. The stretch from 366 to 376 us had 0.66 and 1.00 in the traces of new_again and wqb_behind_exp, whose lists differ in one step 300 us ahead, with TensorE busy 8.29 and 7.70 of 10 us, and the spans, 410.3 and 407.4, differ by 2.9. Where one of them falls on a chain it shows as a wait of VectorE. What decides it stays open; a kernel that keeps TensorE busier there was not tried.
